# A block of linear attention and a gated expert layer: iterations written out, and the transposed x kept in device memory

## What is computed

```
# attention with a positive feature map; 16 heads of width 16, 64 features each
q, k, v = x @ Wq + bq, x @ Wk + bk, x @ Wv + bv        # each split into heads
qp = relu(q @ rw) + 1e-6                               # per head
kp = relu(k @ rw) + 1e-6
kv = sum over s of kp[s] outer v[s];  ks = sum over s of kp[s]      # per batch and head
att = (qp @ kv) / (qp @ ks + 1e-6)
x1 = layernorm(x + att @ Wo + bo)

# expert layer on x1
sim = (x1 @ Wrq) against two sets of 64 keys, 4 heads; the 8 best of each set,
      the 8 best of their 64 sums, softmax over these -> weights over 1024 experts
w = silu(x1 @ down[expert]) * weight;  experts = sum of w * up[expert]
mlp = (silu(x1 @ Wg + bg) * (x1 @ Wu + bu)) @ Wd + bd
y = layernorm(x1 + mlp + experts)
```

## Time and profile before

| | us |
|---|---|
| median of 3 runs | 4005.03 (4003.9 to 4014.2) |
| the profiled execution | 4021.45 |
| its span, first to last instruction | 4019.7 |
| PE busy | 3759.8 (94%) |
| DVE busy | 3012.2 (75%) |
| POOL busy | 1686.0 (42%) |
| ACT busy | 1347.7 (34%) |

### The profile page before, as it was taken

The page is one execution under the profiler, slowest core; times in us unless marked ns, Lnnn a source line. Parts: engine busy times, 40 slices in busy tenths (PEclk is TensorE's granted clock), DMA queues, the critical chain, the costliest instruction groups (busy, mean ns, idle before and its releaser), DMA issues.

```text
span 4019.7 us, 58160 instructions
## 1 busy us (share of the span) xinstructions
PE 3759.8 (94%) x19388; PEld 3133.7 (78%) x19388; DVE 3012.2 (75%) x5947; ACT 1347.7 (34%) x1990; POOL 1686.0 (42%) x1004
## 2 busy tenths in 40 slices
PE   8878999999999999999999999999999999888888
PEld 7757888888787887878788777888877788776776
DVE  2277887777787777877777778777778777888883
ACT  3223333233333333333333333333333333332321
POOL 0044444344443444544344444434444444544541
PEclk7668999999999999999999999999999999999999
DMA  3000000000000000000000000000000000000000
GB/s 106 6 11 11 16 17 11 12 17 11 17 16 17 11 11 17 11 17 17 12 11 16 12 16 17 17 12 11 17 12 17 17 6 11 11 11 7 11 6 11
DMA packets 23384, 61.75 MB, mean 15 GB/s; under 512 B 5552, under 2 KB 10032, under 8 KB 23088
## 3 DMA queue, kind: packets, MB, share of 16 engines
q1 hardware_dynamic: 18480, 41.04, 3.0%
q0 software_dynamic: 4608, 16.78, 1.0%
HBM read 41.04 MB, written 16.78 MB: 14 GB/s over the span
## 4 chain that ended last, share of the span: by engine, by line
PE 70%; DVE 11%; issue 9%; POOL 6%; ACT 4%; DVEq 0%; ACTq 0%; SPq 0%; POOLq 0%; DMA 0%
PE ring L549 19%; PE y_bank L633 9%; PE y_bank L635 8%; POOL grid L391 5%; PE rt_bank L549 4%; PE at_bank L572 4%; PE kv_bank L521 4%; DVE grid L957 4%; PE at_bank L492 3%; PE kv_bank L492 3%; PE at_bank L478 2%; PE kv_bank L516 2%; PE at_bank L563 2%; PE pt_bank L613 2%; PE kv_bank L484 2%
## 5 line engine op out<-in xcount | busy, mean ns | idle before, releaser
L391 POOL TENSOR_TENSOR grid<-ex 128x1024 f32<-128x1024 f32 x512 | 1242.5, 2434 | 527.6 <-ACT ex L755 198.7
L957 DVE SCALAR_TENSOR_TENSOR grid<-grid,best 128x1024 f32<-128x1024 f32 x512 | 703.4, 1374 | 105.6 <-POOL grid L391 104.7
L972 DVE SCALAR_TENSOR_TENSOR prob<-grid,rz,prob 128x1024 f32<-128x1024 f32 x384 | 651.1, 1696 | 8.3
L633 PE MATMUL y_bank<-wd_sb,gate 128*128 128x256 f32 x2048 | 624.1, 387 | 5.3 <-DVE wexp L994 5.3
L635 PE MATMUL y_bank<-up_sb,wexp 128*128 128x256 f32 x2048 | 611.6, 380 | 0.0
L382 POOL TENSOR_SCALAR qp<-qp 128x512 f32<-128x512 f32 x256 | 231.6, 905 | 565.9 <-ACT qp L746 559.8
L549 PE MATMUL ring<-x1T_hl,wg_hl 128*128 128x512 f32 x1536 | 430.0, 416 | 41.2 <-issue 39.2
L549 PE MATMUL ring<-x1T_hl,downT_hl 128*128 128x512 f32 x1536 | 423.9, 412 | 20.8 <-ACT gate L760 20.8
L635 PEld LDWEIGHTS y_bank<-up_sb,wexp 128*128 128x128 f32 x2048 | 391.1, 191 | 53.0
L549 PE MATMUL ring<-x1T_hl,wu_hl 128*128 128x512 f32 x1536 | 428.2, 415 | 0.0
L633 PEld LDWEIGHTS y_bank<-wd_sb,gate 128*128 128x128 f32 x2048 | 356.2, 192 | 47.4 <-issue 19.5
(11 more groups left out here) (122 smaller groups left out, 5825.1 us busy)
## 6 DMA issues: line engine op xcount, KB each, us to landing
xb<-in_L_attn_x SPq DMA_DIRECT2D x34, 512.0 KB, 3.5
out_y<-x POOLq DMA_DIRECT2D x32, 512.0 KB, 3.0
xa<-in_L_attn_x SPq DMA_DIRECT2D x30, 512.0 KB, 3.5
prob<-in_L_ffn_down_embed SPq DMA_DIRECT2D x1, 1024.0 KB, 5.9
prob<-in_L_ffn_Wg SPq DMA_DIRECT2D x1, 1024.0 KB, 8.7
prob<-in_L_ffn_Wu SPq DMA_DIRECT2D x1, 1024.0 KB, 10.5
wd_sb<-in_L_ffn_Wd SPq DMA_DIRECT2D x1, 1024.0 KB, 11.4
up_sb<-in_L_ffn_up_embed SPq DMA_DIRECT2D x1, 1024.0 KB, 11.9
```

Of the source, the lines that this page charges most:

```text
L391: pool.tensor_tensor(grid[:, h % 2], bcast(ex[:, h, 0:NX].unsqueeze(2), [P, NX, NK]), bcast(ex[:, RH + h, 0:NK].unsqueeze(1), [P, NX, NK]) ...
L633: pe.matmul(rows, gate[:, c % 2, t * P:(t + 1) * P], wd_sb[:, c, :], start=(c == 0 and t % 2 == 0), stop=False, skip_group_check=True)
L957: marks["keep", h] = rt_steps.mark(dve.scalar_tensor_tensor(out=g, in0=g, scalar=best[:, h, TOP - 1:TOP], in1=g, op0=ALU.is_ge, op1=ALU.mult))
L972: ins = dve.scalar_tensor_tensor(out=row, in0=g, scalar=rz[:, h:h + 1], in1=row, op0=ALU.mult, op1=ALU.add, accum_out=mass[:, 0:1] if h == ...
```

## The change

- **Schedule.** `schedule` has no loop of the chip any more: a loop of the program that writes the kernel calls the body for iterations 4 to 38, with plain numbers. All semaphore values are constants.
- **Kept transposes.** A tensor `xT_kept` in device memory holds the transposed x of all 32 groups. After the key stage's second `turn` of a group, SP stores `xaT` there (in the filling stage the second lane's as well). The attention stage has no `turn` uses; SP loads `xbT` from `xT_kept` when `wo` 1 of the group before is read, ahead of the load of `xb` in its queue, and PE waits for that load before `q` 0. ACT waits, before it writes `xaT` again, until the store of the group before has landed. For group 0 the load waits until PE is through with the filling stage.
- **Places.** AT_SEQ has 20 uses instead of 22. The tables are built anew: the first use stands at AT_MID[0], so that each use but `next` comes one place earlier than before.
- **The addition of bo.** POOL no longer waits for PE ahead of it, only for the load of `xb`.

```diff
-    AT_SEQ = ([("turn", 0), ("turn", 1), ("q", 0), ("q", 1)] + [("qp", j) for j in range(4)] + [("qkv", 0)]
+    AT_SEQ = ([("q", 0), ("q", 1)] + [("qp", j) for j in range(4)] + [("qkv", 0)]
...
+    xT_kept = nc.dram_tensor("xT_kept", [NG, P, KD, G], F32).ap()
...
-        AT_EARLY = [AT_SEQ[3 * c:3 * c + 1] for c in range(7)] + [[]]
-        AT_MID = [AT_SEQ[3 * c + 1:3 * c + 2] if c < 6 else [] for c in range(7)] + [[]]
-        AT_LATE = [AT_SEQ[3 * c + 2:3 * c + 3] for c in range(6)] + [[], AT_SEQ[-2:]]
-        AT_MID[6] = [("wo", 1)]
+        at_places = [(c, place) for c in range(C - 1) for place in range(3)][1:len(AT_SEQ) - 1]
+        at_place = {at: [use] for at, use in zip(at_places, AT_SEQ)}
+        AT_EARLY, AT_MID, AT_LATE = ([at_place.get((c, place), []) for c in range(C)] for place in range(3))
+        AT_LATE[C - 1] = AT_SEQ[-2:]
...
-            batch_end(0)
-            for it in range(BG, 2 * BG):
-                step(it, it % 2, it // BG)
-            batch_end(1)
-            with eng.Fori(2, B) as b:
-                with eng.Fori(0, BG // 2) as j:
-                    for par in range(2):
-                        step(b * BG + j * 2 + par, par, b)
-                batch_end(b)
...
+            for it in range(BG, NG + LAST_LAG):
+                if it <= NG and it % BG == 0:
+                    batch_end(it // BG - 1)
+                live = [0 <= it - lag < NG for lag in (0, ATTN_LAG, ROUTE_LAG, FFN_LAG, LAST_LAG)]
+                body(it, it % 2, *live, it // BG)
...
+            def keep(lane, i, group):
+                sp.wait_ge(lane.read, i * KV_USES + KV_U["turn", 1] + 1)
+                sp.dma_start(xT_kept[group], lane.xT[:]).then_inc(lane.kept, 16)
...
                     wait(sp, at_read, (m - 1) * AT_USES + AT_U["wo", 1] + 1)
+                    sp.dma_start(xbT, xT_kept[m]).then_inc(xbT_loaded, 16)
                     sp.dma_start(xb[:], x_groups[m]).then_inc(xb_loaded, 16)
+                if kv:
+                    keep(main, in_main(a), a)
...
                     pool.wait_ge(xb_loaded, (m + 1) * 16)
-                    pool.wait_ge(at_full, m * AT_USES + 2)
...
-                    if kind == "turn":
+                    if kind == "q":
                         if j == 0:
-                            pe.wait_ge(xb_loaded, (m + 1) * 16)
-                        mm = turn(at_bank, xb, j)
-                    elif kind == "q":
+                            pe.wait_ge(xbT_loaded, (m + 1) * 16)
                         mm = project(at_bank, wq_sb, xbT, j)
...
+                    if j == 0:
+                        wait(act, lane.kept, i * 16)
```

40 lines of the change are left out of this document (21 added, 19 removed).

## The result

The changed kernel takes 4063.8 us (median of 4 runs, 4061.6 to 4065.5), the kernel before 4009.6 us beside it (4 runs, 4003.9 to 4015.5): a ratio of 1.0135, 95% interval 1.0115 to 1.0154. The profiled execution took 4065.52 us.

A forecast was written before the change was run, and what follows sets the result against it. The prediction held an iteration's first quarter bound by DVE and the PE-ACT-DVE round trips, the rest by PE. Its terms -80 + 40 + 26 - 2 - 10 = -26 us gave 3979 us from 4005.03, range 3910 to 4012 us.

The forecast's parts named there:

- Part 1: Main loop: writing out 25 iterations brings each to 115.5 us, -80 us; -57 us if each takes 116.4 us.
- Part 4: New store and load of 512 KB per group: hidden except at group 0, -2 us, between -6 and +4.
- The walk through the first quarter: Iteration 7 retimed with moved uses: PE waits 2.3, 1.3 and 3.0 us before q1, qp0 and k1.
- its addition to 463.5: DVE's addition after the first keep, before k1: ends at 463.5, with the second keep starting at 464.5.
- part 3: Attention steps one place earlier: k1 starts 1.9 us later, +1.55 us an iteration, +40 us; bounds -23 and +65.
- I take half of the iterations at 2 us: Clock falls to 1.2 GHz behind the wait before k1 in half the iterations: +26 us, bounds 0 and +70.
- part 5: Iterations 32 to 35, without key stage: one branch goes and waits shorten, -10 us, between 0 and -20.
- slower: Rival: clock falls before k1 every iteration and the second grid takes 2.9 us; 120.7 us an iteration, 4043 us, chance 0.09.
- The bias addition lands badly: Rival: bo's addition stops DVE's normalisation of x1 at its new place, 0.9 us an iteration, +23 us, 4002 us, chance 0.07.
- The clock holds: Rival: all as forecast but no clock fall behind the wait before k1, -52 us, 3953 us, chance 0.22.
- the first quarter doesn't get longer: Rival: round trips of q0 and q1 fit and PE gains 0.9 us, -115 us, 3890 us, chance 0.13.
- writing out doesn't remove the idle time: Rival: PE waits for instructions on a straight line too, half of the -80 us stays, about 4019 us, chance 0.04.

The follow-up runs named there:

- experiment 1: The kernel before with only its loops written out, all uses at their old places and both transposes still on PE: 3936.2 us, ratio 0.9797.
- experiment 4: The changed kernel with 20 unused transposes of the identity added in PE's wait before k1: 4012.0 us, ratio 1.0008.
- experiment 12: The changed kernel with ACT's exponential ahead of q1's high parts, output normalisation ahead of q1's low parts, and bo's addition in part 0: 3932.7 us, ratio 0.9792.
- experiment 5: The changed kernel with POOL's small xs step ahead of the first grid instead of between the two grids: 4055.6 us, ratio 1.0102.
- experiment 2: The changed kernel with the attention uses back at their old places, transposes kept and bo's addition still at the end of the iteration before: 3952.1 us, ratio 0.9842.
- experiment 11: The changed kernel with POOL's addition of bo moved into part 0, waiting for DVE's scores: 4039.9 us, ratio 1.0049.
- experiment 7: The changed kernel with attention uses at their old places and POOL's addition of bo moved into part 0, behind DVE's scores: 3925.6 us, ratio 0.9773.
- experiment 3: The kernel before with loops written out, both transposes on PE, no device-memory copy, and all other attention uses one place earlier: 4087.3 us, ratio 1.0172.
- experiment 9: The changed kernel with DVE's output normalisation ahead of q1's low parts in part 0: 4059.7 us, ratio 1.0112.

## Why the prediction was wrong, step by step

**Where it held.** *Part 1, writing out, -80 us:* -81 us in the 26 iterations (3083.8 to 3002.8), -82 in the medians (experiment 1). The Trainium skill, page "Runtime: NRT & Kernel Launch", section "Instruction fetch mechanics", says that "Branching breaks sequential prefetch". The runs agree as far as they can: 3.1 to 3.8 us before the first weight load behind a backward branch, none there on the straight line; what the engine did in that time they don't show. *Part 4, the DMAs:* PE waits for the loaded transposes once, before the very first query projection, the case for which the prediction had "just covered":

```profile
144.92 0.50 PEld L491 LDWEIGHTS at_bank<-qp,wq_sb 128*128 128x128 f32 x2 [1.85 <-DMA qp<-xT_kept]
```

The projection starts no later than in the kernel before (144.92 against 145.61), so the forecast holds in time, though by its own list such a wait was a sign of being wrong. In the steady iterations there is none. The 2 us of this part are in any case far below the scatter of the start (experiment 4).

*The walk through the first quarter* was right up to the first keep: waits of 1.91 and 1.38 us at q1 and qp0 (forecast 2.3 and 1.3), and the exponential, first grid and first keep within 0.2 us of where it had them.

**Step 1 that failed: "its addition to 463.5", part 3.** The addition was taken at 1.0 us. POOL's second grid had moved along with the exponential and began with it: 2.49 us. The second keep then took 1.62 us instead of 1.29, beside POOL's step on qp. So k1 came 2.76 us later than in the kernel of experiment 1, where 1.9 was forecast. Not all of the 1.5 us by which the addition is longer counts, since the prediction already let the second keep wait for the end of the grid: it had the keep start at +21.6, and it starts at +22.0. The addition is worth 0.4 us of the miss, the longer keep 0.3. The prediction had both operations and their times in hand, and put the grid's end against the keep that waits for it, not the grid's run beside what DVE does meanwhile. Its upper bound of +2.5 us was for a longer second grid; that one took 1.90 us as before, and DVE was held in its place. The pairs in the traces: 2.49 us against 0.75 with no grid beside it (experiment 12), 2.91 against 1.28 (experiment 5), 2.10 against 0.40 (experiment 2), 2.03 against 0.42 (experiment 12). Of the Trainium skill's page "SBUF — State Buffer", section "Who interferes with whom", the prediction used the part on VectorE instructions with two SBUF inputs. The addition that was held (L974) and the normalisation of x1 (L928) have one; for them stands another sentence there: a `tensor_scalar` can run in a mode that takes the port shared with GpSimd, and then whoever came first blocks the other. The traces agree that DVE instructions of both kinds are held: each of the four ends 0.15 to 1.1 us behind the POOL instruction beside it. Who came first they leave open: in three of the pairs POOL's began 0.07 to 1.4 us earlier, but at the addition DVE's record begins 0.03 us before POOL's, and it was DVE that was held.

**Step 2 that failed: "I take half of the iterations at 2 us", the clock.** The clock fell at k1 in 26 of 26, each at 1.7 us (experiment 11), or 1.5 by experiment 4: about 40 to 44 us, where 26 was forecast. That the fall follows from the idle PE is shown by experiment 4: with the wait filled and k1 at the same time, it does not come. Taking half from the branches' eight of eleven was the softer error. More than half of the branches had fallen after 3.1 to 3.8 us, and the wait was then longer (3.84, not 3.0). A second fall, near +12, comes in 4 iterations, 3 of them the first of a batch, where q1 waits 2.87 us, the fourth number 23 with 2.22 us; those take 121.6 to 122.1 us instead of 119.5. That second kind was not in the prediction at all.

**The sum of one iteration.** The kernel of experiment 1 has 115.44 us, the changed one 119.46. k1 is 2.76 later and the fall costs 1.70. The bias addition costs 0.18, the difference to the iterations of experiment 11 that fell. Against that, from k1 to the next iteration it takes 0.63 us less, of which qp1, already done, is 0.35; the other 0.3 is not assigned. 2.76 + 1.70 + 0.18 - 0.63 = 4.01. The forecast had 1.55 + 1.0. Times 26 that is 104 us; the iterations with a second fall and other long ones bring it to the measured 120.5.

Over the whole kernel the forecast had -26 us between the profiled executions, and they differ by +44. Of these 70 us, 54 are in part 3 and the clock (120.5 instead of 66), 13 at the end, 4 at the start, and part 1 gained 1 more than forecast. The bounds that the prediction set for part 3 and the clock, +65 and +70, hold the 120.5; its range, up to 4012 us, left that corner out.

**The third step, part 5, the end, -10 us:** +2.5 us. Written out alone it is 5 us shorter (604.5 after iteration 31), and the places take 7.6 of that back (612.1): the wait before qp0 went from 3.62 to 1.37 us, but q1 (2.77 instead of 1.38), the later parts and the last transposes took it over. With the exponential first it is 595.8 us.

**The rivals.** The one marked "slower" is nearest to what happened. Its first half is right, "the wait before k1 sets the clock to 1.2 GHz in every iteration", at 1.7 us instead of 2.7. Its second half, a second grid of 2.9 us, is not: the grid took 1.90 us and DVE was held. So that its 120.7 us an iteration comes so near the measured 120.1 is in part luck. It gave 4043 us. Against the kernel before that is +38; the profiled executions differ by +44, with less lost in the iterations and more at the end and the start. The other 15 us are in the step from one profiled execution to the medians: the one the forecast started from took 16 us more than the median beside it (4021.5 against 4005.0), that of the changed kernel 2 more. The rival had 0.09, because the fall in every iteration and the longer first quarter were counted as two unlikely things on top of one another. They go together: both hang on when k1 starts, and with the exponential early the wait before k1 is 1.3 us in the usual iteration, and no fall follows (experiment 12). *The bias addition lands badly* happened as well: one normalising operation of x1 takes 2.10 us. That its 23 us meet the 24 of experiment 11 is luck: it had 0.9 us an iteration, and in the changed kernel it is 0.18, or 5 us in all; 9 us of the 24 are five iterations in which the clock held. At the old places it does cost 0.9 (experiments 2 and 7). The forecast treated it as an alternative to the main case, and it is an addition to it. *The clock holds*, *the first quarter doesn't get longer* and *writing out doesn't remove the idle time* did not happen.

**The cause, as far as shown.** Experiments 2 and 3 put the loss on the places. Experiment 12 narrows it to a neighbour: moving q1 one place forward on ACT put it ahead of the exponential, so that the exponential waits for q1's whole round trip, and with it the chain of choice, grid, keep, addition, k0's low parts and k1. With the exponential back in front, and the two small moves, 131 us come back. How the roughly 103 us beyond the two moves split when the exponential alone is moved was not tried: experiment 9 gave nothing by itself, and may be worth more once the exponential is early. Not settled either are why the clock held behind k1 in 5 of the 26 iterations of experiment 11, and why it was lower in the filling stage of some executions than of others.

## What to carry to other kernels

When steps are moved one place earlier in a hand-written order, look on each engine at what they have overtaken, and not only at whether their own inputs are ready: here ACT had 2.3 us of idle time, and the exponential that would have filled it stood behind the moved step. A block between DVE and POOL belongs to whatever DVE does at that moment, so a shift of POOL's grid has to be charged to its new neighbour; in experiments 5 and 12 making it earlier only chose another. And terms that hang on the same wait are not independent: here a longer wait before k1 made both the quarter longer and the fall surer, so the corner where both are bad deserved more than 0.09. Compare executions of one kernel by stages before explaining a difference of the medians: here up to 22 us went with the clock in the filling stage.

## What the runs showed of the hardware that was not expected

- Twenty useless transposes in a wait of 3.84 us made the kernel faster by 40 us in 26 iterations: PE then idled 1.51 us before k1 and stayed at 2.4 GHz (experiment 4).
- The same wait of about 3.84 us before k1 is followed by the fall to 1.2 GHz in 26 of 26 iterations of the changed kernel, 21 of experiment 11 and 18 of experiment 3. After 2.07 us it came in no iteration of experiment 1. The wait of 2.9 us before q1 in the first iterations of a batch was followed by one in 3 of 6 cases in the changed kernel, and a wait of 2.3 us in the same place in 3 of 6 in experiment 2.
- Two executions with the same filling stage got a mean clock of 0.77 and 0.88 in their first 125 us, and 520 and 592 products done (changed kernel and experiment 4).
- Of DVE's four normalising operations of 0.40 us only the one beside POOL is held: beside the bias addition, 3.34 us there, it takes 2.10 us, and the three behind it stay as they are (experiment 2).
